# Message stage: VectorE's small chain dealt out between its wide instructions, and one pair's squares moved ahead of ScalarE's roots

## The reference, cut to what matters

```python
x_local_tangent = logmap(x[row], x[col])      # dist * (y + xy * x) / norm
h = silu(cat(x_tangent[row], x_tangent[col], distance) @ att_w1 + att_b1)
att = sigmoid(h @ att_w2 + att_b2)
agg = segment_sum(x_local_tangent * att, row) / NORM_FACTOR
```

## Time and profile before

| what | value |
| --- | --- |
| median of 3 runs | 4218.88 us (4201.57 to 4222.59) |
| profiled execution, from its first to its last instruction (span) | 4137.2 us |
| message stage in the profile, about | 2336 to 3934 us |
| VectorE (DVE) busy over the span | 3401.4 us (82%) |
| TensorE (PE) busy | 3002.7 us (73%) |
| ScalarE (ACT) busy | 2194.8 us (53%) |
| GpSimd (POOL) busy | 1969.1 us (48%) |
| mean granted TensorE clock | 0.889 of full speed |

### The profile page before, as it was taken

One profiled execution on the slowest core, in us unless ns is written; L12 is line 12 of the kernel. 1 busy time (PEld: TensorE's weight loads), 2 busy tenths in 40 slices (PEclk: granted clock), 3 DMA queues, 4 the chain that ended last, 5 costly groups with the idle time before them and its releaser, 6 DMA issues. The chain is left out here.

```text
span 4137.2 us, 55464 instructions
## 1 busy us (share of the span) xinstructions
PE 3002.7 (73%) x12662; PEld 2413.6 (58%) x12662; DVE 3401.4 (82%) x9121; ACT 2194.8 (53%) x5961; POOL 1969.1 (48%) x2404
## 2 busy tenths in 40 slices
PE   3545444577777777677756688988988888888866
PEld 2434333455555555555545567777777777777754
DVE  8999996687888888788878378888888888888877
ACT  3235542444444444444438466666665666666557
POOL 1000003556666666666620366666666666666400
PEclk9867777788998889888988899999999999999988
DMA  2111004666667666666636655655655666556361
GB/s 65 39 55 38 13 26 148 191 202 208 202 208 216 207 209 208 211 205 209 206 98 174 172 161 168 173 163 168 171 168 167 167 172 170 166 167 170 89 145 50
DMA packets 295230, 635.60 MB, mean 154 GB/s; under 512 B 78197, under 2 KB 147123, under 8 KB 294657
## 3 DMA queue, kind: packets, MB, share of 16 engines
q0 software_dynamic: 141312, 463.96, 38.3%
q1 hardware_dynamic: 153602, 168.11, 14.5%
HBM read 587.26 MB, written 44.65 MB: 153 GB/s over the span
## 5 line engine op out<-in xcount | busy, mean ns | idle before, releaser
L2469 POOL DMA_INDIRECT area<-d_xr,col x880 | 890.2, 1012 | 686.8 <-DVE area L2706 236.8
L2562 PE MATMUL ms_near_a<-low,ms_hotT 128*128 x1760 | 550.4, 395 | 204.3 <-issue 99.2
L2066 PE MATMUL at_out<-at_pv,at_hot 128*128 128x264 f32 x1760 | 558.6, 447 | 75.7 <-issue 32.0
L2020 POOL DMA_INDIRECT low<-d_qv,col x440 | 449.6, 1022 | 265.6 <-DVE at_pv L2196 129.1
L2563 PE MATMUL ms_near_c<-tab_c,ms_hotT 128*128 x1760 | 536.1, 387 | 0.0
L2046 PE MATMUL at_kx<-area,tab_c 128*128 x1760 | 508.8, 417 | 21.8 <-issue 20.7
L2562 PEld LDWEIGHTS ms_near_a<-low,ms_hotT 128*128 128x128 f32 x1760 | 327.6, 192 | 301.6 <-issue 258.9
L2066 PEld LDWEIGHTS at_out<-at_pv,at_hot 128*128 128x128 f32 x1760 | 358.9, 217 | 161.9 <-issue 63.1
L2046 PEld LDWEIGHTS at_kx<-area,tab_c 128*128 128x128 f32 x1760 | 372.9, 213 | 96.0 <-issue 25.3
L2238 DVE SCALAR_TENSOR_TENSOR area<-area,tab_c,at_out 128x264 f32 x440 | 211.7, 481 | 216.4 <-remote 114.9
L2604 ACT COPY area<-area 128x2 f32<-128x2 f32 x440 | 82.0, 186 | 566.0 <-DVE area L2675 379.0
(11 more groups left out here) (375 smaller groups left out, 6560.6 us busy)
## 6 DMA issues: line engine op xcount, KB each, us to landing
tab_c<-by_dst_marks SPq DMA_DIRECT2D x110, 512.0 KB
ms_near_no<-by_src_near SPq DMA_DIRECT2D x110, 224.0 KB
area<-d_xr,col POOLq DMA_INDIRECT x880
d_qv<-low SPq DMA_DIRECT2D x10, 1120.0 KB, 5.0
low<-d_qv,col POOLq DMA_INDIRECT x448
d_xr<-mid_hm SPq DMA_DIRECT2D x5, 1128.8 KB, 6.8
first_x<-in_x_dram SPq DMA_DIRECT2D x5, 1120.0 KB
tab_c<-in_x_dram SPq DMA_DIRECT2D x5, 1120.0 KB, 7.0
```

The costliest lines, as they stand in the source:

```text
L2020: pool.indirect_dma_start(out=ring[t.n % SLOTS][:, k, :], out_offset=None, in_=m.d_qv, in_offset=bass.IndirectOffsetOnAxis(ap=col[:, t.h, ...
L2066: last = TE.matmul(out[:, p % 2, 0:AW], hot[:, t.h % 2, j, :], pv[:, t.h % 2, j].rearrange("p h d -> p (h d)"), start=(k == 0), stop=(k == ...
L2469: pool.indirect_dma_start(out=far_rows(t, p)[:, k, :], out_offset=None, in_=m.d_xr, in_offset=bass.IndirectOffsetOnAxis(ap=col[:, t.h, SPA ...
L2562: TE.matmul(near_a[:, (SPAN * p + k) % 4, 0:TW], rows, m.tab_a[:, bass.ds(at, TW)], start=True, stop=True)
```

## The change

The window's small chain (`angles`) is cut into ten functions, one for each step that waits, and `period` calls them one at a time between the wide instructions of `p` = 0, 1 and 2. The pairs of attention sums and of one-hot rows are emitted singly, so that a step can stand between the two. `radii` goes from `p` = 1 to `p` = 2, `shares` from `p` = 2 to `p` = 3, and its reciprocal is put behind the one-hot rows. The semaphore counts of the chain run through the whole stage instead of starting anew for each window. In ScalarE's `period` the squares of pair 1 go ahead of `chain`. The arithmetic is the same, instruction by instruction.

```diff
@@ ScalarE, period @@
                     silu(t, 1)
+                    squares(t, 1)
                     if w:
                         chain(w)
-                    squares(t, 1)
                     silu(t, 2)
@@ VectorE @@
-                def hot_rows(t, p):
+                def hot_row(t, p, i):
...
-                def attention_sums(t, p):
+                def attention_sum(t, p, k):
...
-                def angles(w):
+                links, own = Links(dve, dv), OWN
+                def own_parts(w):
...
+                    for rows, k in groups_of(w):
+                        links.mark(V.tensor_tensor(Q[:, k], rows[:, :, 0], rows[:, :, 0], ALU.mult))
+                        links.mark(V.tensor_tensor(own[:, k], rows[:, :, DIM], FARM[:, w.wslot, k], ALU.subtract))
+                def apart_squares(w):
+                    links.wait()
+                    links.mark(V.tensor_tensor(DD, SQ[:, w.wslot, :], Q, ALU.subtract))
+                def excess(w):
+                    links.wait()
+                    for rows, k in groups_of(w):
+                        links.mark(V.tensor_tensor(E[:, k], DD[:, k], rows[:, :, DIM], ALU.subtract))
...
+                def radicands(w):
+                    links.wait()
                     V.scalar_tensor_tensor(R, T, 1.0, A, ALU.add, ALU.mult).then_inc(ab_in, 1)
+                    links.mark(V.scalar_tensor_tensor(U, A, 2.0, own, ALU.add, ALU.mult))
...
+                def bounded_norms(w):
+                    links.wait()
                     V.tensor_scalar(NN, NN, EPS, None, ALU.max).then_inc(nn_in, 1)
...
                 def period(t):
                     w, old = window_of(t), t.plus(-LATE)
                     for p in range(SG):
+                        before, r = pair_before(t, p, 1)
+                        done, q = pair_before(old, p, 3)
+                        if w and p == 1:
+                            excess(w)
                         differences(t, p)
-                        done, q = pair_before(old, p, 3)
+                        if w and p == 1:
+                            above_one(w)
+                        if w and p == 2:
+                            bounded_norms(w)
                         if done.exists():
                             add(done, q, starts.values(q, 1)[0])
                         if p == 2 and old.exists():
                             starts.fetch(old.n * SG, SG)
-                        attention_sums(*pair_before(t, p, 1))
-                        if p == 0 and w:
-                            angles(w)
+                        if w and p == 1:
+                            less_one(w)
+                        attention_sum(before, r, 0)
+                        if w and p == 1:
+                            radicands(w)
+                        attention_sum(before, r, 1)
+                        if w and p == 0:
+                            own_parts(w)
+                        if w and p == 1:
+                            with_excess(w)
+                        if w and p == 2:
+                            radii(w)
                         if p == 3:
                             hot_columns(t.plus(2))
-                        hot_rows(old, p)
+                        if w and p == 3:
+                            shares(w)
+                        hot_row(old, p, 0)
+                        if w and p == 0:
+                            apart_squares(w)
                         if w and p == 1:
-                            radii(w)
-                        if w and p == 2:
-                            shares(w)
+                            times_rest(w)
+                        hot_row(old, p, 1)
+                        if w and p == 1:
+                            norms(w)
+                        if w and p == 3:
+                            inverse_shares(w)
```

More of the change, by code:

```diff
@@ L2663, in _ @@
                 V = nc.vector
-                PER = 13
                 def differences(t, p):
@@ L2699, in attention_sums @@
-                def attention_sums(t, p):
+                    if i == 0:
+                        if p == 0:
+                            dve.wait_ge(c_ready, t.window + 1)
+                        if t.plus(-1).exists():
+                            dve.wait_ge(out_in, t.plus(-1).n * SG + p + 1)
+                    k = SPAN * p + i
+                    at = (t.h % WG) * G + k
+                    V.tensor_scalar(hot[:, k, :], m.ramp[:, :], col[:, t.h, k, 1:2].bitcast(F32), cs[:, t.wslot, at:at + 1],
+                                    ALU.is_equal, ALU.mult).then_inc(weighted, 1)
@@ L2700, in attention_sums @@
+                def attention_sum(t, p, k):
                     if not t.exists():
                         return
[L2702 to L2707, removed]
+                    if k == 0:
+                        dve.wait_ge(silu_in, t.n * SG + p + 1)
+                    at = (t.h % WG) * G + SPAN * p + k
+                    row = far_rows(t, p)[:, k, XB:XW]
+                    V.tensor_tensor_reduce(out=row, in0=row, in1=r_aw2, scale=1.0, scalar=0.0, op0=ALU.mult, op1=ALU.add,
+                                           accum_out=AL[:, t.wslot, at:at + 1]).then_inc(al_in, 1)
@@ L2717, in add, with groups_of @@
                     V.scalar_tensor_tensor(row, row, keep[:, bass.ds(n, 1)], out[:, p % 2, 0:TW], ALU.mult, ALU.add).then_inc(summed, 1)
-                def angles(w):
+                links, own = Links(dve, dv), OWN
+                def groups_of(w):
+                    return [(dd[t.slot], slice((t.h % WG) * G, (t.h % WG) * G + G)) for t in (w, w.plus(1))]
+                def own_parts(w):
                     n = w.window
-                    ln = Links(dve, dv, n * PER)
-                    sq, own = SQ[:, w.wslot, :], OWN
-                    groups = [(dd[t.slot], slice((t.h % WG) * G, (t.h % WG) * G + G)) for t in (w, w.plus(1))]
                     dve.wait_ge(squared, (w.n + WG) * G)
@@ L2731, in angles @@
                         dve.wait_ge(a_in, WG * n)
[L2732 to L2739, removed]
@@ L2749, in angles @@
-                    ln.wait()
-                    ln.mark(V.tensor_tensor(U, U, A, ALU.mult))
-                    ln.wait()
-                    ln.mark(V.tensor_tensor(NN, U, DD, ALU.add))
-                    ln.wait()
+                    for rows, k in groups_of(w):
[4 more added lines that the diff above has]
+                    links.mark(V.tensor_tensor(DD, SQ[:, w.wslot, :], Q, ALU.subtract))
@@ new lines, in radicands, with with_excess, times_rest @@
+                def radicands(w):
+                    links.wait()
+                    V.scalar_tensor_tensor(R, T, 1.0, A, ALU.add, ALU.mult).then_inc(ab_in, 1)
+                    links.mark(V.scalar_tensor_tensor(U, A, 2.0, own, ALU.add, ALU.mult))
+                def with_excess(w):
+                    links.wait()
+                    links.mark(V.tensor_tensor(U, U, E, ALU.add))
+                def times_rest(w):
+                    links.wait()
+                    links.mark(V.tensor_tensor(U, U, A, ALU.mult))
@@ L2754, in angles, with norms @@
+                def norms(w):
+                    links.wait()
+                    links.mark(V.tensor_tensor(NN, U, DD, ALU.add))
+                def bounded_norms(w):
+                    links.wait()
                     V.tensor_scalar(NN, NN, EPS, None, ALU.max).then_inc(nn_in, 1)
-                    assert ln.n == PER, (ln.n, PER)
                 def radii(w):
```

23 lines of the change are left out of this document (6 added, 17 removed).

## The result

The changed kernel takes 4235.58 us (median of 7 runs, 4223.88 to 4255.16). The kernel before, run beside it, takes 4210.44 us (median of 7, 4189.02 to 4222.59). The ratio is 1.0079 with a 95% interval of 1.0055 to 1.0102, so the change costs 0.8%, about 33 us (the two medians lie 25 us apart). The forecast was 4277 us, 58 us above the 4218.88 of before: the direction was right, the size 25 to 33 us too large.

A forecast was written before the change was run, and what follows sets the result against it. Bound: a ring of waits through VectorE, ScalarE and TensorE, 28.56 us a round. First part +1.87 us, partly given back, so +1.05 over 54 windows: 57 us, 4218.9 to 4276, rounded to 4277; own range 4235 to 4325, wider 4170 to 4375.

The forecast's parts named there:

- ScalarE behind `nn_in`: ScalarE's root of the norm waits for VectorE's last small step; silu of pair 2 ends 1.87 us later.
- VectorE behind it: VectorE reaches the attention sum of pair 2 at 10.15 us and waits 3.1 us there for ScalarE.
- GpSimd: Its gather starts at about 8.4 us of the round, 0.7 us later, costed at nothing.
- late wait: VectorE's idleness at the round's end before the next pair 0, up to 4.37 us, cause unnamed, the main doubt.
- TensorE: Next odd pair starts 1.87 us later; rest ahead of it grows from 0.67 to 2.5 us or more.
- rival in which it slows on top of a second part that stays: Full 1.87 us growth plus TensorE's half pace in half the rounds: 4369 us; chance 0.27 with or without slower clock.
- second part: Round from the end of ScalarE's silu of pair 3 to the next pair 0: mean 15.77 us, predicted 14 to 16.
- I take the middle, +1.05 us: Round's growth between 0.23 and 1.87 us; over 54 windows 57 us; chance of this middle case 0.38.
- first part: Round from VectorE's difference of pair 0 to the end of ScalarE's silu of pair 3: 12.79 us, predicted 14.66.
- +1.87 us: Growth of the first part of each round, from ScalarE's later silus of pairs 2 and 3.
- give-back: Shrinking of the second part that offsets the first part's growth, down to 14.13 us at the nearest row.
- The base: Profiled execution of before, 4137.2 us, plus 81.7 us up to the median of its timed runs, 4218.9 us.

The follow-up runs named there:

- three later comparisons: The unchanged changed kernel timed beside the kernel before, twice on chip 14 and once on chip 9: ratios 1.0117, 1.0097 and 1.0108.
- squares-ahead kernel: Kernel before with only ScalarE's squares of pair 1 moved ahead of its chain, VectorE's chain still one block: 3862.93 us beside 3703.11, ratio 1.0418.
- squares behind: Changed kernel with ScalarE's squares of pair 1 put back behind its chain: ratio 1.078 on chip 4 (3994.51 us), 1.024 on chip 14 (4288.64 us).

## What the prediction had right, and the term that it mis-sized

**ScalarE behind `nn_in`.** Right, nearly to the digit: the last step at 7.36 us where 7.39 was worked out, 0.94 us of idleness ahead of the root where 0.9 was, the silus of pairs 2 and 3 at 13.23 and 14.60 where 13.28 and 14.66 were. From "The DRAIN you can't avoid" in the Trainium skill's "VectorE: DVE Perf Modes" the prediction told only half: the section also says that a next operation which isn't held (made to wait for all earlier VectorE instructions) starts earlier. This trace agrees with that half, and not with the flat rule: 0.08 us to the next instruction in all of the dealt steps shown, which last 0.16 and 0.17 us.

**VectorE behind it.** Right in what came: its work became less, and it waits 2.96 us at pair 2 for ScalarE. Wrong in what it says of the kernel before, "VectorE waits for ScalarE at pair 2 already". In the earlier trace rows the sum at 3067.14 has no idle time ahead of it, and the page's row shown above has no wait for ScalarE: VectorE's own work and ScalarE's silu came to that point within 0.14 us of each other. What made VectorE's saving worthless here was ScalarE's delay, not a wait that was there already. The saving itself was 0.74 us of busy time a round, where 1.19 us of VectorE's time were forecast. Part of the difference is that the 0.03 us between two steps of the block (3060.13 to 3060.16 in the earlier trace rows) were never busy time.

**GpSimd.** Right: the gather behind its first small steps starts 8.57 us into the round at 3237.63, where 8.4 was worked out. It costs nothing: in the rounds of this profile with a late wait the gather's last landing is recorded at least 24 us ahead of the difference.

**TensorE.** Right: it rests 2.5 us and more ahead of the odd pair, and half pace follows in 34 of 51 rounds. The rival in which it slows on top of a second part that stays didn't come true: no round at half pace in any of these profiles has a late wait of over 1 us. In the profile after, the second part has a mean of 14.33 us in the rounds at half pace and 15.93 in the others.

**The term that was mis-sized** is the sum's "I take the middle, +1.05 us", 57 us in all. In the three pairs of profiles at the slower level the round grew by 0.88, 0.81 and 0.49 us. Two assumptions are in that term. The first was that the growth of the first part, "+1.87 us", holds in each round ("if the first is alike everywhere"). The typical first part did grow by nearly that, 1.73 us (medians of 12.88 and 14.61), but its mean only by 1.27 (13.37 to 14.64), and on chip 14 by 1.63 and 1.43. In 5 of 52 rounds of the kernel before, the silu of pair 1 ends at 7.1 us or later instead of 3.4, since TensorE's count reached ScalarE and VectorE late at pair 1 as well. One of them is the very round that the forecast used for the rest of 3.03 us; ScalarE ahead of that silu, and VectorE:

```profile
3206.78 0.19 ACT L2604 COPY area<-area 128x2 f32<-128x2 f32 x1 [3.63 <-remote]
```

```profile
3206.85 0.69 DVE L2672 TENSOR_TENSOR area<-area,ms_near_a 128x514 f32<-128x514 f32 x1 [0.89 <-remote]
```

The changed kernel rests TensorE in each round and has one such round. The second assumption was the give-back. It was the middle between two bounds, with no row behind it, so where it came near it was luck: 0.82 us was forecast, 0.39 came in this pair of profiles, and 0.82 and 0.94 in the two pairs on chip 14. So the growth of the first part was taken too large in all three, and the give-back too large in this pair alone. With both, the round grows by 0.88 us, 54 x 0.88 = 48 us, and the stage in the profile by 56.

**The base.** The time of the profiled execution and the times of the other runs don't differ by "what lies around the span". The runs after give both for each execution: 4231.7 us with a span of 4229.7, so 2 us lie around it. The profiled execution of before, with 4137.2, was some 70 us faster than its timed runs. Its message loop, first to last difference, took 1568.0 us; the later executions of before took 1568.6 and 1592.2, those of after 1624.4, 1615.3, 1624.8 and 1620.8. At this level the mean round of before varies by 0.4 us from one execution to another, that of after by 0.14, and the forecast's working was made against a short one. Of the forecast's 58 us, 48 are what the mean round shows in the profiles. The 15 us from there to 33 are no more than this variation, but no run shows that it is their cause. In the three later comparisons the medians differ by 36 to 48 us, and the ratios correspond to 41 to 48.

**What stays open.** Why TensorE's counts reach VectorE late in a long stretch without rest wasn't found. It's seen that they do so at the slower level, in no run on chip 4, and not at the end of a round at half pace. What the changed kernel costs on a chip like number 4 wasn't measured. An estimate from the rows: its first part of 14.6 us and the second part of 12.4 us, or of 14.1 us with eight matmuls at half pace (both seen in the squares-ahead kernel), give rounds of 27.0 to 28.7 against 25.3, a ratio of 1.025 to 1.05.

## What to carry to other kernels

Before a chain of small steps is spread between wide instructions to save its waits, find who consumes its last result: spreading took 0.7 us a round from the producer's busy time (40 us over 54 windows) and put its last result 2.8 us back. Deal the steps early enough that the last one starts where it did as a block (4.6 us here), and the same edit gains 0.6 to 1.1% instead of losing 1%. And an edit's price depends on its surroundings: the squares moved ahead of the roots cost 2.5 us of the first part alone, and saved 0.8 us behind the deal.

## What was not expected of the hardware

The same program takes 3703 us on one chip and 4141 to 4210 on the others, and 4141 and 4192 in two visits to one chip, with equal durations of single instructions. In the message stage the difference is waiting, VectorE's for TensorE's results: 0.2 us against up to 4.5 us at the end of a round. What makes one visit slow isn't known.

TensorE's granted clock fell to half beside rests. Ahead of the odd pair, the kernel before rests 0.7 us in a typical round, and in 0 or 4 of 51 rounds the clock then falls; those 4 had rested 3.03 us. With rests of 3.3 us (squares behind) it falls in 48 and 50 rounds. In between, the length of the rest doesn't decide alone: the kernel with the squares ahead rests 2.62 us in all 51 rounds and the clock falls in 14. The four profiles of the changed kernel have 60 rounds with a rest of over 3.8 us, all at half pace, and 102 rounds with 2.45 to 2.6 us, of which 45 are. The kernel before also meets the half clock elsewhere in its rounds, 12 to 21 times in 51 rounds at the slower level, each within 4 us of a rest of 1.86 us or more; on chip 4 never.

On chip 4 eight matmuls at half pace lengthened the second part from 12.39 to 14.13 us, and thirteen to 15.32. At the slower level rounds of the changed kernel at half pace typically took the same 14.13, with no late wait behind them. Whether that's a gain differs. In the profile after, the rounds with the late wait had a second part of 16.55 us at the median and a whole round of 30.80 on average, against 28.99 at half pace; the later profile on chip 14 is alike, and on chip 9 it is 30.00 against 29.49. In the first one on chip 14 whole rounds took 29.51 with the late wait and 29.64 at half pace, no gain at all.
